# A selective scan in a four-layer kernel: the sum over the states by accumulating transposes, turned back, with a ring of four PSUM banks in place of five

## The reference, cut to what matters

```python
def _selective_scan(x, dt, A, Bm, Cm):           # x, dt: (b, 2048, 1024), N = 16 states
    def step(h, inp):
        x_t, dt_t, B_t, C_t = inp
        dA = jnp.exp(dt_t[..., None] * A)
        dBx = dt_t[..., None] * B_t[:, None, :] * x_t[..., None]
        h = dA * h + dBx
        y = jnp.einsum('bdn,bn->bd', h, C_t)     # the sum over the 16 states
        return (h, y)
...
ys = _selective_scan(xc, dt, A, Bm, Cm)
y = (ys + D_param[None, :, None] * xc) * jax.nn.silu(z)
return jnp.einsum('bdl,hd->blh', y, out_proj_w)
```

## Time and profile before

| | us |
|---|---|
| median of three runs | 5363.93 |
| lowest and highest | 5358.28, 5369.31 |
| the profiled execution, its own time | 5354.56 |
| its span | 5352.8 |
| `l2_scan`, about 2380 to 4254 of the span | 1870 |
| PE busy in the whole span | 4902.7 (92%) |
| DVE, POOL, ACT busy | 3251.4, 2309.7, 1881.3 |

### The profile page before, as it was taken

How to read it: one execution, slowest core, us unless ns; L and a number is a source line. 1 busy time by engine, 2 the same in 40 slices (tenths; PEclk the granted TensorE clock), 3 DMA queues, 4 the chain that set the end, 5 groups by cost and what they waited for, 6 DMA issues and landing times. The chain is left out here.

```text
span 5352.8 us, 40461 instructions
## 1 busy us (share of the span) xinstructions
PE 4902.7 (92%) x14496; PEld 2349.2 (44%) x14496; DVE 3251.4 (61%) x3534; ACT 1881.3 (35%) x2677; POOL 2309.7 (43%) x1219
## 2 busy tenths in 40 slices
PE   8998989999868899968789999999999999999998
PEld 4443234467536444423333444444444344457443
DVE  1663468756457322239999999999999722103522
ACT  1554620045322111125555555555555410002100
POOL 1003420000022000019999999999999742100421
PEclk8899999999989999989999999999999999999999
DMA  2001030000010121142116436444644320000001
GB/s 75 1 1 67 32 118 24 28 17 1 9 34 1 40 68 67 50 123 53 42 40 174 133 124 179 140 133 134 181 140 124 127 82 0 24 0 27 22 16 47
DMA packets 180006, 360.84 MB, mean 67 GB/s; under 512 B 21790, under 2 KB 56734, under 8 KB 175710
## 3 DMA queue, kind: packets, MB, share of 16 engines
q1 hardware_dynamic: 171742, 330.45, 20.4%
q0 software_dynamic: 8064, 27.80, 1.4%
HBM read 300.50 MB, written 57.67 MB: 67 GB/s over the span
## 5 line engine op out<-in xcount | busy, mean ns | idle before, releaser
L2851 POOL TENSOR_TENSOR l2scan_h<-l2scan_dtx,l2scan_Bb 128x1024 f32<-128x1024 f32 x512 | 1198.2, 2358 | 30.8 <-DMA l2scan_Bb<-l_bc 15.0
L2753 PE MATMUL l2scan_yp<-l2scan_h,ident 128*128 128x512 f32 x2048 | 971.5, 608 | 115.1 <-POOL l2scan_h L2876 101.1
L2820 ACT ACTIVATE l2scan_ring<-l2scan_dt,l2scan_A 128x512 f32<-128x512 f32 x1024 | 663.9, 681 | 639.4 <-DVE l2scan_h L2932 481.0
L2753 PEld LDWEIGHTS l2scan_yp<-l2scan_h,ident 128*128 128x128 f32 x2048 | 389.3, 193 | 639.4 <-issue 481.1
L2743 PE MATMUL l2scan_low_z<-state,l2scan_Wz 128*128 128x512 f32 x1024 | 476.6, 598 | 0.3
L2876 POOL TENSOR_TENSOR l2scan_h<-l2scan_h,l2scan_Cb 128x1024 f32<-128x1024 f32 x192 | 452.1, 2355 | 8.6 <-DVE l2scan_h L2921 0.9
L2411 PE MATMUL l2in_acc<-state,l2in_W 128*128 128x512 f32 x1024 | 444.9, 595 | 10.5 <-DMA l2in_W<-l_attn_in_x 10.5
L2932 DVE TENSOR_TENSOR l2scan_h<-l2scan_ring,l2scan_Cb 128x1024 f32<-128x1024 f32 (+1 forms) x384 | 394.3, 1041 | 6.1 <-DMA l2scan_Cb<-l_bc 0.7
L2921 DVE TENSOR_TENSOR_SCAN l2scan_ring<-l2scan_ring,l2scan_carry,l2scan_h 128x512 f32<-128x512 f32 x320 | 392.7, 1273 | 0.0
L2921 DVE TENSOR_TENSOR_SCAN l2scan_ring<-l2scan_ring,l2scan_h 128x512 f32<-128x512 f32 x320 | 373.3, 1212 | 5.5 <-POOL l2scan_h L2851 5.5
L2538 PE MATMUL l2scan_oacc<-l2scan_oy,l2scan_oW 128*128 128x512 f32 x768 | 353.1, 592 | 0.0
(11 more groups left out here) (409 smaller groups left out, 7538.2 us busy)
## 6 DMA issues: line engine op xcount, KB each, us to landing
l2scan_oy<-l_y SPq DMA_DIRECT2D x192, 512.0 KB, 4.9
l2scan_Wz<-l_attn_in_z SPq DMA_DIRECT2D x64, 512.0 KB, 3.6
l2scan_oW<-l_attn_out_w SPq DMA_DIRECT2D x192, 128.0 KB, 3.3
l_xc<-l2in_xc SPq DMA_DIRECT2D x16, 1024.0 KB, 4.8
l2scan_xc<-l_xc SPq DMA_DIRECT2D x64, 256.0 KB, 5.7
l2scan_Bb<-l_bc SPq DMA_DIRECT2D x128, 128.0 KB, 6.9
l2scan_Cb<-l_bc SPq DMA_DIRECT2D x128, 128.0 KB, 7.8
l_y<-l2scan_zs SPq DMA_DIRECT2D x64, 256.0 KB, 5.5
```

Source lines behind the costliest of these rows:

```text
L2753: last = t.matmul(yp[:, :], K.ident[:, :], h[:, st % SLOTS, j, :], start=g == 0 and j == 0, stop=g == NSG - 1 and j == SGR - 1)
L2820: a.activation(bank(st, j), dt[:, q % 2, :], ACT.Exp, scale=A[:, ct, n:n + 1]).then_inc(dA_ok, 1)
L2851: g_.tensor_tensor(h[:, st % SLOTS], dtx[:, None, :].to_broadcast([P, SGR, NT]), Bb[:, g * SGR:(g + 1) * SGR, :], ALU.mult).then_inc(dBx_o ...
```

## The change

The ring gets four banks. The freed bank is `yT`. `total` no longer multiplies by an identity: for each state it passes the four 128x128 blocks of `h` through TensorE's transposing pass, accumulating over all 16 states of the item in `yT`, so that the transposed sum stands there. A new step `keep` of ACT copies yT to SBUF (`ysb`), a new step `turn_back` of TensorE transposes the four blocks into yp, and `finish` waits for that and moves from behind g = 1 to behind g = 2. `keep` stands on ACT right ahead of `gate`, `turn_back` on TensorE at the head of g = 2. `total` of an item's first step waits for `copied` and no longer for `finish`.

```diff
-    BANKS = 5
+    BANKS = 4
+    BLOCKS = NT // P
...
+        ysb = s.sb("ysb", [P, BLOCKS, P])
+        yT = s.ps("yT", [P, BLOCKS, P])
...
                     if g == 0 and q:
+                        t.wait_ge(copied, q)
+                    for j in range(SGR):
+                        for k in range(BLOCKS):
+                            last = t.matmul(yT[:, k, :], h[:, st % SLOTS, j, k * P:(k + 1) * P], K.ident[:, :], is_transpose=True,
+                                            start=g == 0 and j == 0 and k == 0, stop=g == NSG - 1 and j == SGR - 1 and k == BLOCKS - 1)
+                    last.then_inc(summed, 1)
+
+                def turn_back(q):
+                    t.wait_ge(copied, q + 1)
+                    if q:
                         t.wait_ge(y_ok, q)
-                    for j in range(SGR):
-                        last = t.matmul(yp[:, :], K.ident[:, :], h[:, st % SLOTS, j, :], start=g == 0 and j == 0, stop=g == NSG - 1 and j == SGR - 1)
-                    last.then_inc(summed, 1)
+                    for k in range(BLOCKS):
+                        last = t.transpose(yp[:, k * P:(k + 1) * P], ysb[:, k, :], K.ident[:, :])
+                    last.then_inc(turned_back, 1)
...
                     q, g = divmod(st, NSG)
+                    if g == 2 and q:
+                        turn_back(q - 1)
...
                 total(STEPS - 1)
+                turn_back(ITEMS - 1)
...
+                def keep(q):
+                    a.wait_ge(summed, (q + 1) * NSG)
+                    if q:
+                        a.wait_ge(turned_back, q)
+                    a.activation(ysb[:, :, :], yT[:, :, :], ACT.Copy).then_inc(copied, 1)
...
                     if g == 1 and q:
+                        keep(q - 1)
                         gate(q - 1)
...
+                keep(ITEMS - 1)
                 gate(ITEMS - 1)
...
                 def finish(q):
-                    v.wait_ge(summed, (q + 1) * NSG)
+                    v.wait_ge(turned_back, q + 1)
...
-                    if g == 1 and q:
+                    if g == 2 and q:
                         finish(q - 1)
```

More of the change, by code:

```diff
@@ L2592, in l2_scan @@
         carried_v, carried_g = s.sem("carried_v"), s.sem("carried_g")
-        y_ok = s.sem("y_ok")
+        copied, turned_back, y_ok = s.sem("copied"), s.sem("turned_back"), s.sem("y_ok")
         y_out = [s.sem(f"y_out{j}") for j in range(2)]
```

## The result

| | before | after |
|---|---|---|
| median of four runs, us | 5361.10 | 5419.34 |
| lowest and highest | 5356.14, 5369.31 | 5414.14, 5422.34 |
| span of the profiled execution | 5352.8 | 5418.7 |

The changed kernel is slower: ratio 1.0106, 95% interval 1.0089 to 1.0124. Predicted were 5380 us, with a range from 5354 to 5412. The measured time lies above that range; it is the one of the third rival (5410 to 5425), the low clock that falls into the loop.

What follows compares the result with a forecast made beforehand. PE and POOL were taken to run level in chunk 1, DVE 1% behind. Terms -7 + 13 + 4 + 8 - 3 + 4 = +19 us, taken as +16 on the median 5363.93: 5380 us, range 5354 to 5412.

Steps and rivals of the forecast that it cites:

- the third rival: Chunks 0 and 2: low clock reaches sums of g = 5 to 7 and z; +45 us, 5410 to 5425, chance 0.15.
- PE's relief: Scan sums on PE: 0.88 instead of 1.71 us a step, PE 28.3 to 22.1 us an item in chunk 1.
- The loop: Once an item, POOL, PE, ACT's keep, DVE's g = 2 and finish wait in turn: +13 us chunks 1, 3; +4 chunks 0, 2.
- the prediction's last part: Signs in the profile after: ACT waiting for PE, DVE for ACT, POOL for DVE; items of 28.8 and 29.1 us.
- Clock: PE idling ahead of g = 3's sum lowers its clock at z's first parts, mostly hidden: +4 us, from 0 to 45.
- the second rival: Listed second: in the scan the loop costs half and B's rows arrive in time; 5354 to 5374 us, chance 0.32.
- Four banks: Ring of h: a step's first exponential waits for step st - 2, hidden; doubled DVE instructions go: 0 us.
- The SP queue: Chunk ends: the store waits for the later finish and delays B's loads behind it: +8 us, from 0 to 10.
- the heads: Behind the heads of chunks 1 to 3, POOL waits less for PE's sums: -7 us of 9.8.
- The end: Scan's end: 3.7 us from last product to last multiplication, which stood 6.6 behind: -3 us.
- The first rival: Scan: PE's relief shows and the loop doesn't close; 5350 us (5346 to 5353), chance 0.10.

Runs made afterwards that it cites:

- the filled kernel: The changed kernel with identity matmuls, results unused, added on TensorE ahead of and behind the sum of g = 3: 5380.73 us, ratio 1.0046.
- the kernel filled with transposes: The changed kernel with unused transposing passes added on TensorE around the sum of g = 3, eight in place of each added identity matmul: 5392.40 us, ratio 1.0065.

## Why the prediction was right in its direction and wrong in its size

- **PE's relief.** The accumulating pass goes at 0.109 us as taken: a sum of eight passes takes 0.87 from start to start at full clock (3136.20 to 3137.07 above). PE's busy time in chunk 1 is 83% (near 80 predicted). Right.
- **The loop.** Predicted 28.8 and 29.1 an item with 17 us in all; at full clock (the filled kernel) 28.94 and 29.23, and 22 us. The missing 0.14 in chunk 1 lies in DVE's link with its handing over to POOL (7.56 for 7.45) and in ACT's (4.64 for 4.6), not in z's wait for `pre_dt`, since PE is 1.01 us early there. For chunk 0 the prediction took the shorter recurrences off once, though two pairs stand in the loop; by its own rows it should have said 29.0. Its links were those named: the waits of ACT, DVE and POOL are as the prediction's last part asked for, and moving `keep` with `finish` takes them nearly all away (DVE's wait for ACT from 100.5 to 5.9, POOL's for DVE from 46.9 to 0.6).
- **Clock: the step that failed.** The prediction saw the low stretch come, at the right place and of some length (PE idle 3.5 to 5 us ahead of g = 3's sum: 3.85), and said that it "falls in a slack of 2.8 (the sum of g = 3 and z's first six matmuls take 6.9 of the 9.7 between the products of g = 3 and 5)" (the 6.9 holds the sum of g = 4 too). That slack was worked out from PE's own count and POOL's, and left out what z waits for. z's first part can't start before `pre_dt` has left `low_z`, and `pre_dt` stands on DVE behind the product of g = 4. In the slow item z starts 2.48 after the sum of g = 3, which takes 0.87: 1.6 of the 2.8 are gone, and 1.2 are left. The low stretch costs 2.85 (z's 5.25 in place of 2.58, and 1.05 in place of 0.87 for the sum of g = 4); 1.2 of it found room, and 1.6 came out on the loop. The term was +4 with a range to 45; it measured 32 by the ratios and by the scan's chunks (36 in mid-chunk, since the first items of the filled kernel's chunks are 4 longer in all). The third rival had the mechanism, with a chance of 0.15, and its number was met, but not its place: it put the low stretch past the product of g = 5, in chunks 0 and 2. It lies ahead of it, and it is chunks 1 and 3, where POOL's own count is shortest (28.3), that suffer most (+25.9 and +21.8 against +5.0 and +7.8). The prediction says of slow clock through transposes that it is the second rival; what it bears on is this third one, and the kernel filled with transposes speaks against it.
- **Four banks** 0: right, by a run of its own, within 4 us.
- **The SP queue**, +8 less 7 for the heads. POOL's wait for B rises from 7.7 to 14.0, so +6; the heads' first three items together grow by 2 (predicted +1). The store goes out 10.7 later than in the earlier trace rows, 

```profile
2847.78 0.33 SPq L2679 DMA_DIRECT2D l_y<-l2scan_zs  x1
```

  of which 0.7 is the later start of the scan, 4.7 the chunk's own lengthening and 5.3 the later `finish` (5.5 predicted). Right.
- **The end**, -3. DVE's wait for the last sum falls from 5.83 to

```profile
4314.16 0.76 DVE L2923 SCALAR_TENSOR_TENSOR l2scan_yp<-l2scan_xc,l2scan_Dp,l2scan_yp 128x512 f32<-128x512 f32 x1 [3.77 <-PE l2scan_yp L2766]
4315.42 0.69 DVE L2926 TENSOR_TENSOR l2scan_zs<-l2scan_zs,l2scan_yp 128x512 f32<-128x512 f32 x1 [0.51 <-ACT l2scan_zs L2828]
```

  but ACT's gate now comes last: from the end of the last product to the last multiplication it is 5.0 (6.6 before), -1.6. I had left z's last part on PE (1.72) out of this term.
- **The sum.** Loop 22, clock 36 and heads 2 are the 60.5 of the chunks. The medians differ by 58 and the two profiled spans by 66; the last item with its end takes 0.9 more (its own steps are late too, against the -1.6), and some 4.5 us lie outside the scan, in code that both kernels share. Of these 0.7 are a later start of the scan. Behind the scan a later layer (around L3291) loses 5.5, of which the end gives 1.7 back: there the granted clock is 0.50 in two stretches, 5003.4 to 5013.7 and 5044.4 to 5051.2, where the kernel before has one, 4941.2 to 4948.1. Why the clock falls differently there wasn't tested.
- **The first rival**, that the relief shows and the loop doesn't close (5350), isn't reached by opening the loop alone: 5360.05 with `keep` moved, since POOL's wait for B then rises to 23.6. With the rows of B freed from the store too it is 5339.08, below that rival.

What stays open: why the filling with transposes takes 4 us more in the scan than that with matmuls, and why the clock falls for longer in the later layer of some of the kernels.

## What to carry to other kernels

Work out a slack between two points from every wait in it, not from the busy time of one engine: a bank that holds another operand until someone has read it is a wait too. Taking work off an engine that is level with others can make it idle and so slow it where the next piece is due; look whether that piece is on a loop, and if so take the new step out of the loop (here, a copy behind two exponentials instead of ahead of them) before anything else. When a result is finished later, look at what is queued behind its store.

## What the hardware showed that was not expected

- Transposing passes hold the granted clock at 1.00 in this kernel as matmuls do (chunk 1, where sums and filling are transposes and z, dt and projection are matmuls), and in chunk 0 it rises from 0.50 to 1.00 while PE does transposes alone, 2642.80 to 2652.61.
- In the slow item an idle time of 3.85 us is followed by a stretch of 6.6 us at 1.2 GHz, and in the short item that stretch begins within the idle time; in the slow item it cost 2.85 us of PE's time. The filled kernel keeps 1.00 with an idle time of 0.42 at the same place.
- An fp32 transposing pass that accumulates, 64 of them for an item in one bank (16 onto each block), takes the same 0.109 us as one that doesn't in the earlier trace rows.
